# Products with quads of fields in a recommendation tower, with part of the chunk sums on VectorE

## The reference

```python
ids_x, ids_y = _pair_ids(32)               # all i < j
p = e[:, ids_x, :]; q = e[:, ids_y, :]
pw = einsum('bpi,pij->bpj', p, w)
z = einsum('bpj,bpj->bp', pw, q)           # 2048 x 496
h = concatenate([z, dense_ctx], axis=1)    # 2048 x 512
h = maximum(h @ W_top1 + b_top1, 0)        # 512
h = maximum(h @ W_top2 + b_top2, 0)        # 256
y = h @ W_top3                             # 2048 x 1
```

## Time and profile before

| | us |
|---|---|
| median of three runs | 1137.32 |
| lowest, highest | 1136.27, 1141.85 |
| profiled execution, whole | 1127.72 |
| its span, first to last instruction | 1125.9 |
| VectorE busy in it | 597.6 (53%) |
| ScalarE busy in it | 67.6 (6%) |
| GpSimd busy in it | 483.4 (43%) |
| granted clock of TensorE, mean | 0.924 |

### The profile page before, as it was taken

The page is one execution under the profiler, slowest core; times in us unless marked ns, Lnnn a source line. Parts: engine busy times, 40 slices in busy tenths (PEclk is TensorE's granted clock), DMA queues, the critical chain, the costliest instruction groups (busy, mean ns, idle before and its releaser), DMA issues.

```text
span 1125.9 us, 11138 instructions
## 1 busy us (share of the span) xinstructions
PE 899.1 (80%) x4592; PEld 308.5 (27%) x4592; DVE 597.6 (53%) x512; ACT 67.6 (6%) x109; POOL 483.4 (43%) x516
## 2 busy tenths in 40 slices
PE   0320259999967789999997599999996599999999
PEld 0100013333322223333332133333332133333333
DVE  0100037778734445667774345567863355578880
ACT  0000000000000000000000000000000000100001
POOL 6777546543266625435356625435356632000000
PEclk9985669999987889999998889999998889999999
DMA  9311101100011101000011101000011100000000
GB/s 325 97 27 26 21 15 24 20 17 13 10 20 22 23 11 19 15 15 18 12 19 23 23 10 20 16 14 19 12 19 24 23 9 11 1 1 1 1 1 0
DMA packets 19348, 28.05 MB, mean 25 GB/s; under 512 B 8913, under 2 KB 9681, under 8 KB 18513
## 3 DMA queue, kind: packets, MB, share of 16 engines
q0 software_dynamic: 16384, 16.81, 8.1%
q1 hardware_dynamic: 2914, 10.53, 2.6%
HBM read 27.30 MB, written 0.01 MB: 24 GB/s over the span
## 4 chain that ended last, share of the span: by engine, by line
PE 70%; another core or an unknown queue 19%; DVE 5%; issue 3%; ACT 1%; DMA 1%; POOL 1%; DVEq 0%; POOLq 0%
PE main_ps L240 37%; PE z_ps L254 21%; PE x_ps L287 6%; DVE prod L312 5%; PE x_ps L223 3%; PE main_ps L287 2%; PE main_ps L241 2%; ACT e_t L323 1%; POOL emb L187 1%; DMA emb<-in_tbl,idx 1%; PE z_ps L258 0%; DMA idx<-in_ids 0%; DVEq L114 0%; ACT ctx_y L342 0%
## 5 line engine op out<-in xcount | busy, mean ns | idle before, releaser
L312 DVE TENSOR_TENSOR prod<-main_ps,e_t 128x1024 f32<-128x1024 f32 x512 | 597.6, 1218 | 500.3 <-PE main_ps L241 258.3
L187 POOL DMA_INDIRECT emb<-in_tbl,idx x512 | 483.2, 944 | 453.5 <-PE x_ps L223 244.4
L240 PE MATMUL main_ps<-e_t,w_sb 64*128 64x512 f32 x1024 | 512.3, 632 | 189.8 <-DVE prod L312 83.2
L241 PE MATMUL main_ps<-e_t,w_sb 64*128 64x512 f32 x1024 | 512.4, 632 | 0.0
L240 PEld LDWEIGHTS main_ps<-e_t,w_sb 64*128 64x128 f32 x1024 | 181.4, 192 | 465.8 <-issue 258.0
L254 PE MATMUL z_ps<-prod,const_sb 128*32 128x512 f32 x2048 | 264.9, 638 | 0.3 <-DVE prod L312 0.3
L241 PEld LDWEIGHTS main_ps<-e_t,w_sb 64*128 64x128 f32 x1024 | 181.1, 192 | 0.0
L254 PEld LDWEIGHTS z_ps<-prod,const_sb 128*32 128x32 f32 x2048 | 55.7, 114 | 192.8 <-issue 136.4
L323 ACT ACTIVATE e_t<-x_ps 128x512 f32<-128x512 f32 x64 | 38.2, 597 | 681.7 <-PE x_ps L223 341.5
L223 PE MATMUL x_ps<-const_sb,emb 128*128 128x128 f32 x256 | 44.5, 299 | 34.3 <-DMA emb<-in_tbl,idx 31.7
L223 PEld LDWEIGHTS x_ps<-const_sb,emb 128*128 128x128 f32 x256 | 28.6, 148 | 89.8 <-issue 75.0
(11 more groups left out here) (10 smaller groups left out, 11.8 us busy)
## 6 DMA issues: line engine op xcount, KB each, us to landing
emb<-in_tbl,idx POOLq DMA_INDIRECT x512
w_sb<-in_w SPq DMA_DIRECT2D x5, 1280.0 KB
w_sb<-in_w SPq DMA_DIRECT2D x1, 1024.0 KB
w_sb<-in_w SPq DMA_DIRECT2D x1, 512.0 KB
w_sb<-in_w SPq DMA_DIRECT2D x1, 448.0 KB
w_sb<-in_w SPq DMA_DIRECT2D x1, 384.0 KB
w_sb<-in_w SPq DMA_DIRECT2D x1, 320.0 KB
w_sb<-in_w SPq DMA_DIRECT2D x1, 256.0 KB, 3.4
```

Of the source, the lines that this page charges most:

```text
L187: pool.indirect_dma_start(out=emb[:, n % G_SLOTS, s, odd * EMBED:(odd + 1) * EMBED], out_offset=None, in_=tables[f], in_offset=bass.Indire ...
L240: nc.tensor.matmul(main_ps[:, slot, :], w_sb[LOW, u, :], even[LOW, 0, :], start=True, stop=True)
L241: nc.tensor.matmul(main_ps[:, slot + 1, :], w_sb[UP, u, :], odd[UP, 0, :], start=True, stop=True)\
L312: nc.vector.tensor_tensor(prod[:, s:s + 2, :], main_ps[:, slot:slot + 2, :], e_q, ALU.mult)\
```

## The change

A *quad* is four neighbouring fields, two duos. The 64 features of each of its fields are cut in halves of 32, so 4 x 32 features fill 128 partitions: a *low* tile with the first halves and a *high* tile with the second. Where duo m meets a quad that lies above it, unit ("low", m, q) computes for each field of the duo the first 32 features of the four pair products, and unit ("high", m, q) the second 32. Pairs between the two duos of one quad stay as before ("duo"), and each comes with a "twin" unit that holds the pairs within both duos. There are again 128 units per tile in 32 rounds, and a round holds two units and then their two second halves: four chunks and then four chunks that go to the same rows of `z_ps`.

In 24 of the 32 rounds all units are of quads. Every other one of these (rounds 2, 5, 8, 11, 13, 16, 18, 20, 24, 26, 28, 30) is *folded*: VectorE adds the high chunks to the low chunks in one instruction of 128x2048 elements, behind the second product of the next round, and TensorE sums only four chunks. The order of TensorE is unchanged: the sum of round r stands behind the fourth unit of round r + 1.

ScalarE writes the quad tiles from `x_ps`, four copies of 32 partitions in front of the copy of the duo, for duos 2 to 15. The slots of `e_t` go from 24 to 8, and there are eight quad slots. The dense features no longer go through TensorE: SP copies 16 rows per tile into `z_sb` behind the evictions of `z_ps`, the first MLP step waits for them, and y is stored tile by tile. Some due times move. `PAST` is 1 and `DMA_FOLDS` is empty.

```diff
+def order_pieces():
+    pieces = []
+    for m in range(DUOS - 1, 1, -1):
+        if m % 2 == 0:
+            pieces.append(("duo", m, m + 1))
+        pieces += [("low", m, q) for q in range(QUADS - 1, m // 2, -1)]
+    pieces.insert(len(pieces) - 2, ("duo", 0, 1))
+    return pieces + [("low", m, q) for q in range(QUADS - 1, 0, -1) for m in (1, 0)]
+
+SECOND = {"duo": "twin", "low": "high"}
+for _r in range(ROUNDS):
+    _two = PIECES[2 * _r:2 * _r + 2]
+    UNITS += _two + [(SECOND[_k], _a, _b) for _k, _a, _b in _two]
+PAST = 1
-E_SLOTS = 24
+E_SLOTS = 8
+Q_SLOTS = 8
+FULL = [r for r in range(ROUNDS) if all(PIECES[2 * r + h][0] == "low" for h in range(2))]
+DVE_FOLDS, DMA_FOLDS = FULL[::2], []
...
-DUO_ROUNDS = (-4, -3, -2, -1, 0, 1, 2, 5, 7, 9, 11, 13, 16, 19, 22, 25)
-MLP_ROUNDS = (3, 4, 6, 8, 10, 12, 14)
+DUO_ROUNDS = (-4, -3, -2, -1, 0, 1, 2, 4, 6, 8, 10, 13, 16, 19, 21, 22)
+MLP_ROUNDS = (3, 5, 7, 9, 11, 12, 14)
...
@@ sync
+            for t in range(TILES):
+                for kt in range(KTILES):
+                    if CTX_ROWS[kt]:
+                        sp.wait_ge(z_out, KTILES * t + kt + 1)
+                    for row, f in CTX_ROWS[kt]:
+                        sp.dma_start(z_sb[row:row + 1, kt, :], ctx_t[f:f + 1, t * TILE:(t + 1) * TILE]).then_inc(ctx_in, 16)
+                if t > 0:
+                    sp.wait_ge(evicted, EVICTED["mlp", t - 1, MLP_STEPS - 1])
+                    sp.dma_start(out[:, (t - 1) * TILE:t * TILE], y_sb[:, :]).then_inc(y_out, 16)
...
@@ tensor, reduce_round
-                for k in range(2 * ROUND):
...
-                if r == ROUNDS - 1:
-                    for g in range(4):
-                        last = nc.tensor.matmul(z_ps[32 * g:32 * g + 32, :], ctx_sel[:, g, :],
-                                                ctx_sb[:, t * TILE:(t + 1) * TILE], start=False, stop=True)
+                if r in DVE_FOLDS:
+                    pe.wait_ge(folded, len(DVE_FOLDS) * t + DVE_FOLDS.index(r) + 1)
...
+                for p in range(2 if r in DVE_FOLDS or r in DMA_FOLDS else ROUND):
+                    kind, slot = UNITS[ROUND * r + p][0], 2 * ((NUNIT * t + ROUND * r + p) % P_SLOTS)
+                    for x in range(2):
+                        g = 2 * (p % 2) + x
...
+                        last = nc.tensor.matmul(z_ps[32 * g:32 * g + 32, :], lhs, prod[:, slot + x, :], start=(rr == 0 and p < 2),
...
@@ vector
-                    e_q = e_duo(t, m + 1, 2) if m == q else e_duo(t, q).to_broadcast([P, 2, TILE])
+                    if kind == "twin":
+                        e_q = e_duo(t, q, 2)
+                    elif kind == "duo":
+                        e_q = e_duo(t, q).to_broadcast([P, 2, TILE])
+                    else:
+                        h = int(kind == "high")
+                        e_q = quad_t[:, quad_slot(t, q), h:h + 1, :].to_broadcast([P, 2, TILE])
...
+                    if u % ROUND == 1 and n >= ROUND and (u // ROUND - 1) % ROUNDS in DVE_FOLDS:
+                        dve.wait_ge(products, n - 1)
+                        s = 2 * ((n - ROUND - 1) % P_SLOTS)
+                        low, high = prod[:, s:s + ROUND, :], prod[:, s + ROUND:s + 2 * ROUND, :]
+                        nc.vector.tensor_tensor(low, low, high, ALU.add).then_inc(folded, 1)
...
@@ scalar, keep_duo
+                q = m // 2
+                if q > 0:
+                    gone, r = divmod((QUADS - 1) * t + QUADS - 1 - q - Q_SLOTS, QUADS - 1)
+                    if gone >= 0 and m % 2:
+                        act.wait_ge(products, NUNIT * gone + FINAL_OF_QUAD[QUADS - 1 - r] + 1)
+                    for h in range(2):
+                        for x in range(2):
+                            rows, to = EMBED * x + HALF * h, EMBED * (m % 2) + BLOCK * x
+                            nc.scalar.activation(quad_t[to:to + BLOCK, quad_slot(t, q), h, :], x_ps[rows:rows + HALF, :], ACT.Copy)
                 nc.scalar.activation(e_duo(t, m)[:, 0, :], x_ps[:, :], ACT.Copy).then_inc(evicted, 1)
```

More of the change, by code:

```diff
@@ L20, in pair_index, with duos_of, moved_of @@
     return i * (FIELDS - 1) - i * (i - 1) // 2 + j - i - 1
[L25 to L31, removed]
-NUNIT = len(UNITS)
[L33 to L36, removed]
+def order_pieces():
[7 more added lines that the diff above has]
+SECOND = {"duo": "twin", "low": "high"}
+PIECES = order_pieces()
+ROUND = 4
+ROUNDS = 2 * len(PIECES) // ROUND
+UNITS = []
+for _r in range(ROUNDS):
+    _two = PIECES[2 * _r:2 * _r + 2]
+    UNITS += _two + [(SECOND[_k], _a, _b) for _k, _a, _b in _two]
+NUNIT = len(UNITS)
+def duos_of(u):
+    kind, m, q = UNITS[u]
+    return (m, q) if kind in ("duo", "twin") else (m, 2 * q, 2 * q + 1)
+def moved_of(u):
+    kind, m, q = UNITS[u]
+    return (m, q) if kind in ("duo", "twin") else (m,)
+FIRST_OF_DUO = [min(u for u in range(NUNIT) if m in duos_of(u)) for m in range(DUOS)]
+FINAL_OF_DUO = [max(u for u in range(NUNIT) if m in moved_of(u)) for m in range(DUOS)]
+FINAL_OF_QUAD = [max((u for u, (k, _, q) in enumerate(UNITS) if k == "high" and q == Q), default=-1) for Q in range(QUADS)]
 ROUNDS_KT = ROUNDS // KTILES
@@ L97, in order_events @@
                         ev.append(("z", r // ROUNDS, r % ROUNDS // ROUNDS_KT))
-    ev += [("reduce", TILES - 1, ROUNDS - 1), ("z", TILES - 1, KTILES - 1)]
+    ev += [("reduce", TILES - 1, ROUNDS - k) for k in range(PAST, 0, -1)] + [("z", TILES - 1, KTILES - 1)]
     return ev + [("mlp", TILES - 1, n) for n in range(MLP_STEPS)]
@@ L154, in dlrm_tower @@
         products = sem("products")
+        folded = sem("folded")
+        dma_folded = [sem(f"dma_folded{k}") for k in range(3)]
         reduced = sem("reduced")
@@ L303, in _ @@
             for t in range(TILES):
-                for u, (m, q) in enumerate(UNITS):
+                for u, (kind, m, q) in enumerate(UNITS):
                     n = NUNIT * t + u
@@ L313, in _ @@
                       .then_inc(products, 1)
+                    if u % ROUND == 1 and n >= ROUND and (u // ROUND - 1) % ROUNDS in DVE_FOLDS:
[3 more added lines that the diff above has]
+                        nc.vector.tensor_tensor(low, low, high, ALU.add).then_inc(folded, 1)
+            if ROUNDS - 1 in DVE_FOLDS:
+                dve.wait_ge(products, NUNIT * TILES)
+                s = 2 * ((NUNIT * TILES - ROUND) % P_SLOTS)
+                low, high = prod[:, s:s + ROUND, :], prod[:, s + ROUND:s + 2 * ROUND, :]
+                nc.vector.tensor_tensor(low, low, high, ALU.add).then_inc(folded, 1)
         @block.scalar
@@ L341, in mlp @@
                 else:
-                    ins = nc.scalar.activation(y_sb[:, t * TILE:(t + 1) * TILE], bank[0:1, :], ACT.Copy)
+                    if t > 0:
+                        act.wait_ge(y_out, 16 * t)
+                    ins = nc.scalar.activation(y_sb[:, :], bank[0:1, :], ACT.Copy)
                 ins.then_inc(evicted, 1)
@@ L361 @@
     a = {k: np.asarray(v) for k, v in inputs.items()}
[L362 to L363 removed]
+    const = np.zeros((P, P + 122), np.float32)
     const[:, :P] = np.eye(P, dtype=np.float32)
@@ L385 @@
         "w": w,
-        "w1": a["W_top1"][rows].reshape(KTILES, P, HID1).transpose(1, 0, 2),
+        "w1": a["W_top1"][W1_ROWS].reshape(KTILES, P, HID1).transpose(1, 0, 2),
         "w2": a["W_top2"].reshape(HID1 // P, P, HID2).transpose(1, 0, 2),
```

100 lines of the change are left out of this document (57 added, 43 removed).

## The result

The changed kernel takes 1239.85 us (median of four runs, 1238.62 to 1243.87) against 1138.43 us of the kernel before on the same chip (four runs). The ratio is 1.0894, 95% interval 1.0855 to 1.0933: 101 us slower. The forecast was 1215, slower by 78. The sign and the range held; the size was too small, and the experiments show that three of its terms were wrong in size. A few executions of the experiments stood far apart from the others of their kernel and are left out of the ratios: 1373.56 us in the half fold (median of its other three 1161.82), 1850.40 in "no folds, spread" and 1203.18 of the kernel before.

A forecast was written before the change was run, and what follows sets the result against it. TensorE paces plain rounds; late releases during GpSimd's gather bursts stretch boundaries and start. Terms 66 − 7 + 5 + 15 − 2 + 1 = +78 on 1127.7 gave 1205.7, raised to 1215 us by the runs' 0.85%; range 1155 to 1258.

The forecast's parts named there:

- likeliest case: Whole kernel: TensorE's waits for folds outweigh the shorter sums, giving 1215 us, own range 1190 to 1235, chance 0.50.
- Place of the fold and its wait: Folded sums: TensorE waits 2.24 us for VectorE's fold and saves 0.86, net +1.38 per fold, 66 us for 48.
- rival B: Fold on VectorE takes only 1.22 us since both inputs are in SBUF: 1167 us in all, chance 0.12.
- Hidden folds (−7): Ten folds in boundary stretches and the start, where GpSimd sets the pace: half counted as hidden, −7 us.
- rival D: TensorE after fold pauses: main products run at 1.2 GHz, up to 3.4 us each; 1260 us, chance 0.10.
- Merged burst (+15): Duos 1 and 0 due in rounds 21 and 22: GpSimd issues 16 gathers on end, +15 us, bounds 0 and 22.
- Evictions (+5): ScalarE copies five times per transpose, releasing duos 2 to 15 2.24 us later; +5 us, mainly first tile, bounds 0 and 31.
- Boundary stretches and start: Around tile boundaries transposes stay where they stood; at the start fewer duos precede GpSimd's pause: 0, start bounds −12 and +15.
- context: Dense features leave TensorE, dropping 8 records of line 258 per tile; one tile's lie in the tail: −2 us.
- tail: End of the last tile: the last fold delays products 126 and 127, so the last sum starts later: +1 us.
- Rival C: Folds and GpSimd gathers contend for SBUF, making folds wait: +8 to +40 us, about 1235 us, chance 0.15.
- Rival A: Boundary and start waits shrink as the new order shifts TensorE's releases against gather bursts: 1095 us, faster, chance 0.08.

The follow-up runs named there:

- half fold: Changed kernel with the fold adding 128x1024 elements, half of the folded rounds' second-half chunks left out of the sum: 1164.36 us, ratio 1.0317 to the kernel before.
- no folds, spread: Changed kernel with all sums in eight chunks and three of the last four duos due a round earlier: 1132.96 us, ratio 1.0029 to the kernel before.
- third set: Four variants, including the changed kernel itself, measured together beside the kernel before, which took 1129.31 us; the changed kernel took 1231.06 us there.
- busy waits: Changed kernel plus eight zero-block products on TensorE before each wait for a fold: 963.79 us (ratio 1.0653), and 1189.45 us (1.0516) where the kernel before took 1129.31.
- no folds: Changed kernel with all sums in eight chunks, everything else kept: 1160.14 us, ratio 1.0277; repeated at 1160.46 us, ratio 1.0272 to the kernel before.
- second set: Four variants measured together beside the kernel before, which took 904.09 us there, not 1130.
- earlier transposes: Changed kernel with folds in their own round, last duos spread, and first-tile transposes of duos 8 to 0 three units ahead, not one: 895.46 us, ratio 0.99.
- last kernel of the third set: Changed kernel with folds in their own round, last duos spread and first-tile transposes three units ahead: 1131.66 us, ratio 1.0009 to the kernel before.
- early and spread kernel: Changed kernel with folds behind the fourth product of their own round and three of the last four duos due a round earlier: 899.46 us, ratio 0.9941.

## Why the prediction was right, and where not

The account of the third set is 31.1 (all but the folds) + 29.0 (folds with the clock kept) + 41.6 (clock) = 101.7 us, against 19 + 59 + 0 = 78. The measured time lies outside the likeliest case's own range (1190 to 1235). That it lies in the stated range (1155 to 1258) owes something to luck: the folds came out 30 us too dear and the clock and the bursts 54 too cheap.

- *Place of the fold and its wait:* right, and with a fold of 2283 ns rival B (a quick fold) is out. 2.17 us against 2.24, 12.36 us for a pair of rounds as computed, in MLP rounds too. In the last tile, r2 to r31, 11 waits of 2.24 and 12 savings of 0.86 make +14.3; busy waits against no folds gave 195.6 − 181.4 = 14.2.
- *Hidden folds (−7):* mis-sized. The folds at kept clock cost 29 us, not 59, so about 30 us more are hidden: in tile 0, r2 to r27, the wait's price would be 9 × 2.24 − 10 × 0.86 = 11.6, and it measured −2.6 (182.6 against 185.2). In tile 1, r20 to r27, it would be +1.9, and it measured −3.2 (49.7 against 52.9). So the late releases under gather bursts set the pace in all of tile 0 and behind round 20 as well, and not only in the start and the boundaries. Where releases came in time (second set) busy waits were 59.7 us above before, near the unhidden sum, though no kernel without folds ran there.
- *Clock (rival D, given 0.10):* the step that failed. The sum puts it at nothing; measured are 41.6 us, 37 without the earlier starts. As a rival its total was priced well (a third of 130 us), by 3.4 us a fold where 1.66 was measured. It was held for a rival, since no gatherless round had a pause before. The earlier trace rows had shown the pattern: a pause of 2.27 us and a record of 1.06 us. With the 24 falls at 1.66 us that were measured, the sum would have been 1215 + 40 = 1255.
- *Merged burst (+15):* mis-sized; 27 us, 12 each in tiles 1 and 2 in the one round with 15 gathers on end, so above the bound of 22 taken from the earlier trace rows.
- *Evictions (+5):* four copies cost 587 ns each, as taken. 4 us were won back by earlier transposes in the second set. Not separated: tile 0, r2 to r27, is 27 us longer than before even without folds (185.2 against 158.4), of which about 11 come back in the start and the stretch behind it. It is unit order, copies and shifted bursts together.
- *Boundary stretches and start (0), context (−2), tail (+1):* start 163.5 and 160.8, boundaries 80.4 to 88.6 before and 83.2 to 83.7 after. Nothing speaks against them within what these vary; the −2 and +1 were not tested by themselves.
- *Rival C:* the contention is there, in the other direction: folds lengthen gathers by 24 us in all. Six of the 19 lie in the stretches around tile boundaries, which took 83.2 to 83.7 us with folds and 80.8 to 82.0 without, so it costs little there; in the last kernel of the third set it goes with bursts that merge again. Rival A (a faster kernel) didn't come.

## What to carry to other kernels

Moving work from the busier engine to an idler one pays by where its result is needed, not by the busy shares: the same 48 instructions cost 70 us where the result came 2.2 us after TensorE needed it, and gained 33 us when issued two products earlier. Count the pause itself as a cost of TensorE's clock: waits of 2.2 us and more in front of a sum came in half the cases with a fall that cost about 1.6 us of slow records, which here cost more than the wait net of its saving. And gather bursts that merge through changed due times want a price of their own: here 27 us for three due times that differ by one round, lost or won in one round per tile by whether 15 gathers ran on end or 7 and 8 with a pause.

## What the runs showed of the hardware that was not expected

The kernel before took 1129 to 1138 us in three sets and 904 us in one (all eight runs within 0.2%), unchanged. The kernel with busy waits ran in both conditions (963.79 and 1189.45 us), and the difference lies where gathers run on end: start to r2 took 79.5 and 161.7 us, the boundaries 50.3 and 82.4 to 85.1, rounds 20 to 27 of tiles 0 to 2 from 41.3 to 42.7 and from 49.4 to 55.2, but rounds 14 to 20 of tile 3 39.4 in both. VectorE in the start of the changed kernel (first) and of the early and spread kernel in the quick set (second), both while GpSimd issued a gather each 1.25 us:

```profile
92.11 1.22 DVE L371 TENSOR_TENSOR prod<-main_ps,e_t 128x1024 f32<-128x1024 f32 x1 [21.87 <-issue]
102.61 1.22 DVE L371 TENSOR_TENSOR prod<-main_ps,quad_t 128x1024 f32<-128x1024 f32 x1 [9.28 <-remote]
113.81 1.22 DVE L371 TENSOR_TENSOR prod<-main_ps,e_t 128x1024 f32<-128x1024 f32 x1 [9.98 <-remote]
```
```profile
41.40 1.23 DVE L371 TENSOR_TENSOR prod<-main_ps,quad_t 128x1024 f32<-128x1024 f32 x1 [5.60 <-PE main_ps L286]
43.10 1.23 DVE L371 TENSOR_TENSOR prod<-main_ps,e_t 128x1024 f32<-128x1024 f32 x1 [0.48 <-PE main_ps L286]
44.24 1.22 DVE L371 TENSOR_TENSOR prod<-main_ps,quad_t 128x1024 f32<-128x1024 f32 x1
```

In the first the releases arrive about 11 us apart, in the second with the products. What decides between the two stays open: both levels were recorded under the same chip number, and each held for its whole set. The best kernel gains 1.0% where releases come in time and nothing measurable where they don't, so a gain found in one condition has to be measured in the other too. What the changed kernel itself takes in the quick condition was not measured.
